# A cross-attention pipeline in which projections run two steps ahead of the maxima instead of three

## What is computed

```
q = x @ Wq.T + bq                      # 128 queries, 16 heads of 16
k = ctx @ Wk.T + bk                    # 12544 keys of 256
v = ctx @ Wv.T + bv
attn = softmax(q k^T / 4)              # over all 12544 keys, for each head
x1 = x + (attn v) @ Wo.T + bo          # then: linear attention, causal attention, 8 experts (top 2)
```

## Time and profile before

| | |
|---|---|
| median of 3 runs | 553.39 us (551.66 to 556.53) |
| the profiled execution: its own time | 553.16 us |
| its span, first to last instruction | 551.3 us |
| mean granted TensorE clock in it | 0.972 |
| busy: TensorE, VectorE, ScalarE, GpSimd | 93%, 70%, 63%, 16% |

### The profile page before, as it was taken

How to read it: one execution, slowest core, us unless ns; L and a number is a source line. 1 busy time by engine, 2 the same in 40 slices (tenths; PEclk the granted TensorE clock), 3 DMA queues, 4 the chain that set the end, 5 groups by cost and what they waited for, 6 DMA issues and landing times.

```text
span 551.3 us, 19593 instructions
## 1 busy us (share of the span) xinstructions
PE 510.8 (93%) x8408; PEld 463.8 (84%) x8408; DVE 386.3 (70%) x712; ACT 346.5 (63%) x688; POOL 90.1 (16%) x75
## 2 busy tenths in 40 slices
PE   7898969999999999999999999999877889776997
PEld 7887859999999999999999999999766778555886
DVE  5488846787777778777787778777664137847574
ACT  3422747778777887878787887877566710072563
POOL 5751100111011111111111111110000000043000
PEclk9999999999999999999999999999899999868899
DMA  5999995979887796988789796976840059900000
GB/s 191 158 154 155 170 191 80 148 123 146 140 130 138 121 159 118 150 130 136 144 125 146 121 153 119 143 121 97 133 148 3 3 184 372 360 2 1 1 1 10
DMA packets 44630, 70.65 MB, mean 128 GB/s; under 512 B 6784, under 2 KB 15104, under 8 KB 44416
## 3 DMA queue, kind: packets, MB, share of 16 engines
q1 hardware_dynamic: 44304, 69.02, 67.5%
q10 hardware_dynamic: 240, 0.39, 0.5%
HBM read 30.53 MB, written 0.13 MB: 56 GB/s over the span
## 4 chain that ended last, share of the span: by engine, by line
PE 82%; DVE 8%; ACT 4%; issue 3%; DMA 1%; SPq 1%; POOL 0%; ACTq 0%; DVEq 0%
PE weighted L753 16%; PE scores L736 15%; PE bank L611 12%; PE bank L629 12%; PE maxima L663 10%; PE scores L1030 3%; ACT probs L424 2%; PE maxima L1014 2%; PE scores L761 2%; PE bank L1014 2%; PE scores L783 1%; DVE stepmax L1119 1%; DMA kT<-kst 1%; PE bank L558 1%; PE bank L578 1%
## 5 line engine op out<-in xcount | busy, mean ns | idle before, releaser
L1127 DVE TENSOR_REDUCE stepmax<-maxima 128x2 f32<-128x512 f32 x340 | 222.8, 688 | 82.6 <-PE maxima L663 79.3
L424 ACT ACTIVATE probs<-scores 128x512 f32<-128x512 f32 x382 | 207.2, 596 | 91.3 <-PE scores L736 91.1
L611 PE MATMUL bank<-cparts,wk 64*128 64x256 f32 x1104 | 178.5, 289 | 1.5 <-DVE kst L1110 0.9
L629 PE MATMUL bank<-wv,cparts 64*128 64x256 f32 x1104 | 172.5, 288 | 0.4
L611 PEld LDWEIGHTS bank<-cparts,wk 64*128 64x128 f32 x1104 | 146.6, 188 | 2.9 <-DVE kst L1110 1.8
L629 PEld LDWEIGHTS bank<-wv,cparts 64*128 64x128 f32 x1104 | 146.4, 187 | 1.5 <-PE bank L629 1.5
L736 PE MATMUL scores<-qmat,kT 64*128 64x128 f32 x1528 | 115.2, 267 | 11.7 <-ACT probs L424 9.3
L736 PEld LDWEIGHTS scores<-qmat,kT 64*128 64x128 f32 x1528 | 103.9, 188 | 16.7 <-ACT probs L424 12.2
L663 PE MATMUL maxima<-kT,qM 64*128 64x256 f32 x680 | 108.5, 306 | 3.9 <-issue 2.7
L338 POOL TENSOR_TENSOR cparts<-ctxT,cparts 128x512 fp32r<-128x512 f32 x49 | 62.9, 1283 | 294.9 <-ACT cparts L384 294.9
L753 PE MATMUL weighted<-probs,val 128*17 128x128 f32 x3136 | 98.1, 278 | 0.0
(11 more groups left out here) (224 smaller groups left out, 417.4 us busy)
## 6 DMA issues: line engine op xcount, KB each, us to landing
kT<-kst SPq DMA_DIRECT2D x291, 128.0 KB, 4.7
ctxT<-in_ctxT SPq DMA_DIRECT2D x49, 256.0 KB, 6.9
w<-in_w SPq DMA_DIRECT2D x24, 512.0 KB, 10.1
bias<-in_biases SPq DMA_DIRECT2D x1, 1024.0 KB, 8.3
kT<-kst ACTq DMA_DIRECT2D x3, 128.0 KB, 5.1
qmat<-maxT SPq DMA_DIRECT2D x24, 8.0 KB
w_xk<-in_w_xk SPq DMA_DIRECT2D x1, 256.0 KB, 2.8
w_xq<-in_w_xq SPq DMA_DIRECT2D x1, 256.0 KB, 3.6
```

The lines of the kernel that those rows point to most:

```text
L424: act.activation(probs[k % PROBS][:, :, :], (late_bank if n >= NS - LAG else sc_bank)[score_banks(k - q % 2)[q % 2]][:, :].rearrange("p (h ...
L611: last = pe.matmul(k_bank[:, cols], wk[rows, pw, c, t * P:(t + 1) * P], cparts[n % 2][rows, pc, c, :], start=not swapped and i == 0, stop= ...
L629: last = pe.matmul(v_bank[:, cols], cparts[n % 2][rows, pc, c, j * P:(j + 1) * P], wv[rows, pw, c, :], start=not swapped and i == 0, stop= ...
L1127: dve.tensor_reduce(heads[:, 2 * m:2 * m + 2], bank[:, :].rearrange("p (i k) -> p i k", i=2), AX_X, ALU.max).then_inc(S["mx_read"], 1)
```

## The change

A constant LEAD = 2 takes the place of the fixed three. Step t projects t + 2. Only two projections stand before the loop. `keys_high` and `keys_low` make keys t + 1 in step t, and SyncE places keys t + 1 in step t, now ahead of the row maxima. TensorE waits for keys t + 1 at the last swapped product (i == 11) of the projection of t + 2. In the first five steps there the maxima wait for their own keys, behind twelve filling products and six rounds of the projection. Step 46 now projects too, so steps 47 and 48 are the late ones. The 1 MB of biases is loaded in eight rows of 128 KB in steps 14, 16, ..., 28, the three small loads in step 32. In steps 47 and 48 the first scores go ahead of the weighted values; from step 49 on, the first half of the weighted values of a step follows its own scores, and the two turned blocks of a step stand apart.

The diff, cut; what is left out renames 3 to LEAD and changes the counts of waits to match:

```diff
@@ -28,7 +28,7 @@
 RING = 8
 VRING = 10
 CRING = 4
-EARLY = 3
+LEAD = 2
 UNITS = 8
 EARLY_UNITS = 4
 GROUPS = 4
...
+LATE_LOADS = [3 * BS + 2 + BS // 2 * i for i in range(8)]
...
@@ -295,16 +297,20 @@
             for t in range(-2, NS + 1):
                 if CRING <= t + 6 < NS:
                     ctx_load(t + 6)
+                if 0 <= t + LEAD - 1 < NS:
+                    keys_place(t + LEAD - 1)
                 for b in range(NB):
                     if t == last_step(b) + 1:
                         max_rows(b)
-                if t + 2 < NS:
-                    keys_place(t + 2)
-                if t == LAG:
-                    sp.dma_start(biases[:, early:], dr["biases"][early:].partition_broadcast(P)).then_inc(S["ld_small"], 16)
+                row = LATE_LOADS.index(t) + 2 if t in LATE_LOADS else None
+                if row is not None:
+                    sp.dma_start(biases[:, row * D:(row + 1) * D], dr["biases"][row * D:(row + 1) * D].partition_broadcast(P)
+                                 ).then_inc(S["ld_small"], 16)
+                if t == LATE_LOADS[-1] + BS:
                     sp.dma_start(router[:, :, :], dr["router"].rearrange("(c p) n -> p c n", p=P)).then_inc(S["ld_small"], 16)
                     sp.dma_start(freqs[:, :], dr["freqs"][0:P, :]).then_inc(S["ld_small"], 16)
                     sp.dma_start(const[:, P:], dr["const"][:, P:]).then_inc(S["ld_small"], 16)
+
                 if t == NS - 2:
 
                     sp.wait_ge(S["k_done"], NS)
@@ -446,15 +452,12 @@
             act.wait_ge(S["ld_v"], 16)
             act.activation(wv[:, 0, :, :], w["xv"][:, :, :], ACT.Copy).then_inc(S["act_wkvh"], 1)
             first_keys_half()
-            keys_high(1)
             act.wait_ge(S["pool_setup"], 1)
             act.wait_ge(S["pe_qT"], 2)
             act.activation(qM[:, PAIRS // 2:PAIRS, :], mx_bank[1][:, :].rearrange("p (h q) -> p h q", q=P), ACT.Copy
                            ).then_inc(S["act_q0"], 1)
+            context_high(2)
             values_out(0)
-            context_high(2)
-            values_out(1)
-            context_high(3)
             for t in range(LAST + 2):
                 n = t - LAG
                 if t == NS:
@@ -462,11 +465,11 @@
                     act.wait_ge(S["dve_dmax"], 1)
                     act.activation(bweight[:, :, :], bweight[:, :, :], ACT.Exp).then_inc(S["act_bw"], 1)
                     part_out(NB - 2)
-                if t + 2 < NS:
-                    keys_high(t + 2)
-                    values_out(t + 2)
-                if t + 4 < NS:
-                    context_high(t + 4)
+                if t + LEAD - 1 < NS:
+                    keys_high(t + LEAD - 1)
+                    values_out(t + LEAD - 1)
+                if t + LEAD + 1 < NS:
+                    context_high(t + LEAD + 1)
                 for b in range(NB - 1):
                     if t == last_step(b) + 1:
                         max_turned(b)
...
@@ -605,9 +608,9 @@
                 if not swapped and i == 0:
                     pe.wait_ge(S["kl_ready"], n)
                 if swapped and i == 0:
-                    pe.wait_ge(S["k_half"], n - EARLY + 1)
-                if swapped and i == 8:
-                    keys_placed(n - 2)
+                    pe.wait_ge(S["k_half"], n - LEAD + 1)
+                if swapped and i == 11 and n - LEAD + 1 >= LAG:
+                    keys_placed(n - LEAD + 1)
                 last = pe.matmul(k_bank[:, cols], wk[rows, pw, c, t * P:(t + 1) * P], cparts[n % 2][rows, pc, c, :],
                                  start=not swapped and i == 0, stop=swapped and i % 6 == 5, skip_group_check=True)
...
@@ -669,8 +672,8 @@
 
 
                 unit = units_ahead(n) + m
-                if m == 0 and n == 0:
-                    keys_placed(0)
+                if m == 0:
+                    keys_placed(n)
                 if unit >= 2:
                     pe.wait_ge(S["mx_read"], unit - 1)
...
-                    if i == 0 and m == 0:
-                        pe.wait_ge(S["cl_ready"], n + 4)
...
-                if m == 0 and n + 2 >= NS:
+                if m == 0 and n + LEAD - 1 >= NS:
...
@@ -811,33 +812,30 @@
                 for j in range(2):
                     for half in range(2):
                         values(n, j, half)
-            for t in range(2):
-                for half in range(2):
-                    keys(2, t, half)
             pe.wait_ge(S["dve_q0"], 1)
             pe.wait_ge(S["act_q0"], 1)
-            for j in range(2):
-                for half in range(2):
-                    values(2, j, half)
             for t in range(LAST + 2):
                 n = t - LAG
                 if t < LAG:
-                    early_maxima(t, 0)
-                    early_maxima(t, 1)
                     for b in range(NB - 1):
                         if t == last_step(b) + 1:
                             turn_max(b)
                     fill(12)
-                    project_both(t + 3, False, 0, 6)
+                    pe.wait_ge(S["cl_ready"], t + LEAD + 1)
+                    project_both(t + LEAD, False, 0, 6)
+                    early_maxima(t, 0)
+                    early_maxima(t, 1)
+                    project_both(t + LEAD, False, 6, 12)
+                    project_both(t + LEAD, True, 0, 4)
                     early_maxima(t, 2)
-                    project_both(t + 3, False, 6, 12)
-                    project_both(t + 3, True, 0, 4)
+                    project_both(t + LEAD, True, 4, 12)
                     early_maxima(t, 3)
-                    project_both(t + 3, True, 4, 12)
                     continue
                 if t < NS:
                     maxima_both(t, 0)
-                    if t + 3 > NS:
+                    if t + LEAD >= NS:
+                        scores(n, 0)
+                    if t + LEAD > NS:
                         maxima_both(t, 1)
                     if n >= 1:
...
-                        if t + 3 == NS:
+                        if t + LEAD == NS:
                             maxima_both(t, 1)
-                        scores(n, 0)
+                        scores(n, 1)
                         maxima_both(t, 2)
-                        scores(n, 1)
+                        scores(n, 2)
                         maxima_both(t, 3)
-                        scores(n, 2)
                         scores(n, 3)
                     continue
                 if t == NS:
...
@@ -885,18 +882,20 @@
                     weighted_values(n - 1, 1)
                     turn_part(2)
                     turn_part(3)
+                part = 4 + 2 * (t - NS)
                 if n < NS:
                     scores(n, 0)
                     scores(n, 1)
                 if t > NS:
-                    weighted_values(n - 1, 0)
                     weighted_values(n - 1, 1)
                 if n < NS:
-                    for b in range(4 + 2 * (t - NS), 6 + 2 * (t - NS)):
-                        if b < NB - 1:
-                            turn_part(b)
+                    if part < NB - 1:
+                        turn_part(part)
                     scores(n, 2)
                     scores(n, 3)
+                    weighted_values(n, 0)
+                    if part + 1 < NB - 1:
+                        turn_part(part + 1)
             turn_part(NB - 1)
             keep_busy(8)
             pe.wait_ge(S["dve_att"], 1)
...
@@ -1179,7 +1178,6 @@
             dve.wait_ge(S["pe_qT"], 1)
             dve.tensor_copy(qM[:, 0:PAIRS // 2, :], mx_bank[0][:, :].rearrange("p (h q) -> p h q", q=P)
                             ).then_inc(S["dve_q0"], 1)
-            keys_low(1)
             for t in range(NS + 1):
                 for b in range(NB):
                     if t == last_step(b) + 1:
@@ -1187,18 +1185,17 @@
                 if t == NS:
                     last_max_turned()
                 if t < LAG:
-                    early_max(t, 0)
-                    keys_low(t + 2)
-                    for m in range(1, EARLY_UNITS):
+                    keys_low(t + LEAD - 1)
+                    for m in range(EARLY_UNITS):
                         early_max(t, m)
                 elif t < NS:
                     for u in range(UNITS):
                         step_max(t, u)
-                        if u == 1 and t + 2 < NS:
-                            keys_low(t + 2)
-
-
-            dve.wait_ge(S["ld_small"], 64)
+                        if u == 1 and t + LEAD - 1 < NS:
+                            keys_low(t + LEAD - 1)
```

More of the change, by code:

```diff
@@ L621, in values_product @@
                 if not swapped and i == 0:
-                    turned = [b for b in range(NB - 1) if last_step(b) == n - 4]
+                    turned = [b for b in range(NB - 1) if last_step(b) == n - LEAD - 1]
                     if turned:
@@ L627, in values_product @@
                 if swapped and i == 0:
-                    pe.wait_ge(S["v_half"], n - EARLY + 1)
```

(33 more changed lines are left out.)

8 lines of the change are left out of this document (4 added, 4 removed).

## The result

The changed kernel took 701.25 us (median of 4 runs, 699.04 to 703.46) beside 554.96 us for the kernel before (551.66 to 563.19) in the same comparison: a ratio of 1.266, with a 95% interval of 1.257 to 1.275. It is slower by a quarter. The forecast was 710 us with a range of 670 to 763.

The account below looks back on a forecast made before the run. TensorE's work bounded each 7.84 us step; after the change the keys' path would. Span terms 62.5 + 491.4 + 11.7 + 7.0 + 135.4 = 708.0 us, plus 1.9 around it, gave 710 us, range 670 to 763.

Parts of the forecast that it names:

- The loop of the keys' path: Steps 5 to 46: last projection product to placed keys repeats every step, 11.7 us each, 491.4 us in all, +152.5.
- L: Time from the end of the keys' low part to the last landing of six key transfers: 9.0 us, bounds 8.2 to 9.9.
- Transfer time, not issue time: Key batch: landings 1.3 us apart against issues 0.64 us apart, so each 128 KB is limited by the transfer.
- Keys in time: Rival for full steps: keys land within 5.1 us of the low part, not slower, about 548 us; chance 0.04.
- The lighter queue: Rival for the key batch: landings follow the issues in a longer step, 9.3 us a step, 607 us; chance 0.08.
- The clock: Rival: TensorE's clock stays low, its 7.84 us of work per step become 15.7, 882 us; chance 0.06.
- First steps: Before step 5: keys come later in a loop spanning two steps; step 5 starts at 62.5 against 56.33, +6.2 us.
- Step 47: Must also wait for the keys of 48: 11.7 us in place of 8.6, +3.1.
- Step 48: Late step, taken to stay at 7.0 us as before the change.
- Last steps: After 410.89 us: weighted values moved among the scores starve ScalarE less, 5 us gained (0 to 7.5), 135.4 us left.
- TensorE's busy share: Sign in the changed kernel's profile: near 75%, with waits for keys of 3 to 5 us in each step.
- the bias load: 1 MB load in step 5 put beside TensorE's 2.72 us stall and a late key batch; no such stall expected after.

Follow-up runs that it names:

- the low part first: Changed kernel with VectorE cutting the low part of the keys ahead of the step's first two maxima instead of behind them: 677.29 us, ratio 1.214 to the kernel before.
- the wait three rounds earlier: Changed kernel with TensorE's wait for the keys back at i == 8 of the second half instead of i == 11: 722.55 us, ratio 1.315 to the kernel before.
- half the bytes: Changed kernel with each of a step's six key transfers moving 64 KB, half its columns: 588.12 us, ratio 1.052 to the kernel before.
- two queues: Changed kernel with three of a step's six key transfers issued by ScalarE beside SyncE's three: 692.91 us, ratio 1.243 to the kernel before.
- twice the partitions: Changed kernel with four of the six key transfers written to 32 partitions instead of 16, same bytes: 653.85 us, ratio 1.174 to the kernel before.
- last and late steps edited: Kernel before with the changed order from step 49 on and, in steps 46 to 48, first scores ahead of weighted values: 544.27 us, ratio 0.983.
- the last steps alone: Kernel before with only the order from step 49 on changed, half the weighted values behind the step's own scores: 548.65 us, ratio 0.995.
- the loads spread: Kernel before with only the late loads changed, 1 MB in eight rows and the small loads in step 32: 552.91 us, ratio 1.005.
- the five loads: Kernel before with the whole 1 MB bias load issued in steps 5, 13, 21, 29 and 37 instead of once: 561.74 us, ratio 0.995.

## Why the prediction was right, and where it wasn't

- **The loop of the keys' path: right.** Step starts are 11.4 us apart, the wait is in each step, and it ends with the landing. Forecast 42 x 11.7 = 491.4 us, measured 478.9. The path up to the low part was put at 2.63 us and 0.1 for the restart; the two together are 2.67 at the upper clock, 2.77 on the mean. Moving one piece of it by -0.53 or +0.47 us moved the step by as much (the low part first, the wait three rounds earlier).
- **L: right in kind, mis-sized by 0.4 us.** Forecast 9.0 of a range of 8.2 to 9.9, measured 8.62 (8.2 to 9.2). I had leaned to the batch behind a wait; the batches after the change lie with the other two. The step came out 0.3 us shorter, 42 x 0.3 = 12.5 us in the loop; step 48 and the first steps, below, took 3 us of that back.
- **Transfer time, not issue time: right,** by half the bytes and by two queues. My step from first to last landing, 1.3 us for each 128 KB, was too large: in a batch of the changed kernel, issued from 306.2 to 309.4, landings come 3.3 us after the issue at least and 5.3 at most, so if the first is the shortest and the last the longest, they are (309.4 + 5.3 - 306.2 - 3.3) / 5 = 1.04 us apart, 126 GB/s. Over 41 batches of this trace, taken singly, it is 1.04 us too.

```profile
L267 SPq DMA_DIRECT2D kT<-kst x6: 547/596/607, 306.2 to 309.4; - x6
...
DMA to landing us min/median/max: 3.3/4.5/5.3
```

  The Trainium skill ("SBUF — State Buffer", section "Door 1: The DMA port swizzle") gives 104 to 109 GB/s for 16 partitions and lets the rate follow the ports that the partitions reach. The trace agrees in direction alone: the measured 126 GB/s is the higher, and twice the partitions brought the landings from 1.04 to 0.95 us apart. So the forecast was right that the transfer is the limit, but the number of partitions, which it named as the reason, explains little of it; the bytes explain more. The Trainium skill ("SBUF — State Buffer", section "Can I just issue two DMAs to hit both halves?") also says that two transfers on the two halves go one behind the other, with 6% gained. My theory for the two queues went against that, and the runs agree with what the Trainium skill says: L fell from 8.62 to 8.3 us, 4%.
- **Rivals.** Keys in time would need L of 5.1 us or less: none came near (least 8.2). The lighter queue (607 us) didn't come, since the bytes of the batch limit it in a longer step too. The clock: it falls and returns, with 0.50 at the restart in a third of the turns and 1.00 in the others. The Trainium skill ("TensorE: Matmul & The Clock Gate", section "HAM oscillation") has a loop that waits in each turn fall in every one of them; the trace agrees in a third. But in the steady steps it costs 4 us of 701, for nearly all the slow products run beside the landings. It did not stay low. Forecast: perhaps 0.3 us of a step; measured: 0.3 us in a third of the steps.
- **First steps:** forecast 62.5, measured 63.67, in part by luck. The loop over two steps is there in the chain (four reductions of 4.62 us together, the low part, the batch), but its batches took 9.1 and 8.5 us where 10.0 stood in the forecast, and 1.8 us of a block's row maximum on VectorE (50.6 to 52.4 us) was not counted. **Step 47:** 11.7 and 11.2. **Step 48:** forecast 7.0, measured 8.9. I had left it as it was, but it begins at a lower clock: from 541.90 to 563.00 the mean granted clock is 0.75, and the weighted values of step 48 take 3.54 us on the chain where they take 1.87 in the earlier trace rows. This term failed by 1.9 us.

```profile
541.90:563.00 21.10, 14.05 (x228) 11.51 (x229) 10.91 (x19) 9.09 (x18) 0.00 (x0) 0.75 0.64 162
```

- **Last steps:** a step of 582.56 - 577.31 = 5.25 us, as forecast (nearer 5.3 than 6.29). In the changed kernel the rest is 135.7 us where 135.4 were forecast. Put alone into the kernel before, the same order brought 2.6 us (0 to 5) where the forecast had 5.
- **TensorE's busy share:** forecast 75%, measured 81%. The old busy time, 93% of 551.3 us, over the new span would be 72 to 73%; at the lower clock the products last longer. So TensorE stood still for less than I said: the waits for keys were put at 3 to 5 us each and are 90.7 / 43 = 2.1 us on the mean, 3.6 at most. ScalarE's 351.5 and VectorE's 387.7 us are, as forecast, nearly those of before (63% and 70% of the span of the earlier trace rows are 347 and 386).
- **A reading that was wrong without harm.** At 80.74 in the earlier trace rows TensorE restarts with a product of the scores; the wait for keys stands before a product of the projection. So what ended there was not a wait for the keys but a stall of the kind below, and that a landing fell at 80.7 too proves nothing about the keys. The other example, the landing at 41.40, stands on the chain and was enough for the step.
- **Another: the bias load.** I put the stalls of the earlier trace rows beside it and said that they would go. Spread, the load gained nothing that can be measured, and five-fold it cost nothing. The sum didn't suffer, since I had counted no gain beyond the 338.9 us.

**The stalls that no semaphore ends.** Stalls of TensorE of 2 to 3 us stand in the profiles with their ends at 72.3 (2.72) and 80.7 (2.20) before, 71.9 (2.84) with last and late steps edited, 134.3 (1.93) with the last steps alone; none is as long with the loads spread. They stand after a large load in some profiles and far from one in another, and no run was made to test their cause. But the kept traces show what they have in common. The kernel before, from its start to the first and to the second of them (products of PE, weight loads of PEld), and its queue of instructions:

```profile
0.00:69.62 69.62, 61.83 (x731) 56.68 (x731) 48.56 (x78) 27.69 (x56) 31.28 (x29) 1.00 0.95 168
0.00:78.54 78.54, 68.03 (x859) 62.26 (x859) 53.17 (x86) 32.46 (x66) 32.57 (x30) 1.00 0.96 171
...
q8 instruction: 65, 1.06, 1.0%
```

Between the two lie 128 products and 128 weight loads, 256 instructions. Counted through all of TensorE's instructions, the stalls named here, the three of the five loads and the one of 1.32 us begin behind instruction 1474, 1730, 4034 or 4290, each a multiple of 256 from the others. The queue moves 65 packets of 16 KB, about one for each 256 of TensorE's 16966 instructions. Before the end of each stall one such packet has run (69.64 to 70.67 us and 77.90 to 79.23 us in the kernel before), and TensorE restarts 1.3 to 1.8 us behind its end. So by these traces TensorE waits there for its next 256 instructions, which also explains a stall between two products of one line.

**What stays open.** Why such a packet comes late in one profile and in time in another is not shown; the 1 MB load may delay one, but the stall at 134.3 us stands some 70 us behind the only such load of its kernel. What within a transfer sets its 1.04 us, beside its bytes, is not shown either. And no run moved the 256 KB of context that SyncE issues behind each batch (at 322.19 us behind keys from 317.34 on) and that land with its last keys; the landings at the end of a batch are closer together (0.86 us) than at its start (1.19), so nothing shows that they slow it.

## What to carry to other kernels

Before a stage is moved nearer to its use, follow its product once around, from the instruction that frees it to the landing that is waited for, and compare that path with the new distance: 11.4 us of path in a step of 7.84 is paid in every step, not once, since the wait holds up the next turn's start. What shortens such a loop is only what lies on it: here the bytes of the transfers and the order of the instructions ahead of them. A second queue brought 0.3 us of 11.4, and a higher clock on TensorE (0.99 in place of 0.89) no time that can be measured. And a bundle of edits is worth taking apart: here one of them cost about 150 us, and the others together brought 2.5%.

## What was not expected of the hardware

- Six transfers of 128 KB that write 16 partitions each land 1.0 us apart on the mean, whether one queue issues them over 3.2 us or two queues over 1.5 us (1.04 and 0.99 us; L 8.62 and 8.3 us).
- The same bytes written by four of six transfers to 32 partitions took 1.0 us off the batch, not the 1.6 expected; half the bytes took off 2.4 us.
- The granted clock of TensorE fell to 0.50 behind a wait in a third of the turns, and this cost 4 us of 701 in the steady steps, since the slow products ran beside the landings.
- TensorE can stand still for 1.3 to 2.8 us with no semaphore to wait for, even between two products of one line: each time a multiple of 256 instructions apart, and until 1.3 to 1.8 us after a 16 KB packet of the instruction queue has ended.
